# Attention and soft-mixture feed-forward on one core: the sums of the slots in three passes over high and low parts, in place of fp32

## What is computed

```python
x = layernorm(x + attention(x))            # x: 8 batches x 1024 tokens x 128
# feed-forward, per batch:
xn = rms_norm(x, gamma_x)                  # 1024 x 128
se = rms_norm(slot_embeds, gamma_slot)     # 512 slots x 128
logits = einsum('bsd,etd->bset', xn, se)   # 1024 tokens x 512 slots
dispatch = softmax(logits, axis=1)         # over the tokens
slots = einsum('bsd,bset->betd', xn, dispatch)
h = gelu(slots @ w1); processed = h @ w2   # 128 -> 512 -> 128
combine = softmax(logits, over the slots)
out = einsum('bnd,bsn->bsd', processed, combine)
x = layernorm(x + out)
```

## Time and profile before

| what | value |
|---|---|
| median of 3 runs | 1963.05 us (1960.64 to 1964.24) |
| the profiled execution's own time | 1951.72 us |
| its span | 1949.9 us |
| PE busy over the span | 1777.2 us (91%) |
| DVE busy | 1577.5 us (81%) |
| ACT busy | 1240.9 us (64%) |
| POOL busy | 1081.5 us (55%) |
| one steady feed-forward batch | 41.44 us |

### The profile page before, as it was taken

The page is one execution under the profiler, slowest core; times in us unless marked ns, Lnnn a source line. Parts: engine busy times, 40 slices in busy tenths (PEclk is TensorE's granted clock), DMA queues, the critical chain, the costliest instruction groups (busy, mean ns, idle before and its releaser), DMA issues. The chain is left out here.

```text
span 1949.9 us, 33601 instructions
## 1 busy us (share of the span) xinstructions
PE 1777.2 (91%) x10556; PEld 1527.5 (78%) x10556; DVE 1577.5 (81%) x2926; ACT 1240.9 (64%) x2450; POOL 1081.5 (55%) x661
## 2 busy tenths in 40 slices
PE   4899989998999899989998999899999949999997
PEld 4788877887788778867887888688888837878886
DVE  3879987997899778978997789788889856777674
ACT  2767766776777667756776677577767615445553
POOL 3556655664666556555665556566656433455543
PEclk7999999999999999999999999999999979999999
DMA  3322232223222322232223222322233120111100
GB/s 105 80 60 82 66 87 57 75 66 89 66 66 66 87 66 66 66 89 66 66 66 87 66 66 66 87 66 66 74 82 82 48 81 22 46 42 32 35 19 22
DMA packets 69767, 127.90 MB, mean 66 GB/s; under 512 B 15456, under 2 KB 42080, under 8 KB 69600
## 3 DMA queue, kind: packets, MB, share of 16 engines
q1 hardware_dynamic: 68416, 124.81, 23.5%
q10 hardware_dynamic: 1184, 1.05, 0.2%
HBM read 50.07 MB, written 8.65 MB: 30 GB/s over the span
## 5 line engine op out<-in xcount | busy, mean ns | idle before, releaser
L448 ACT ACTIVATE probs<-ps_slot,neg_max 128x640 f32<-128x640 f32 (+7 forms) x512 | 379.1, 742 | 172.7 <-DVE neg_max L533 165.2
L533 DVE CUSTOM_DVE_ANT_0 ps_slot<-ps_slot,causal 128x640 f32<-128x640 f32 (+7 forms) x512 | 385.5, 753 | 39.5 <-PE ps_slot L57 38.5
L681 PE MATMUL ps_turn<-ident,probs 128*128 128x128 f32 x2304 | 339.0, 278 | 54.6 <-DVE pt_high L564 34.7
L681 PEld LDWEIGHTS ps_turn<-ident,probs 128*128 128x128 f32 x2304 | 264.9, 142 | 95.3 <-DVE pt_high L564 37.9
L55 PE MATMUL ps_slot<-k,q 128*128 128x512 f32 (+3 forms) x768 | 284.1, 370 | 39.3 <-DVE rot_q L549 38.6
L412 POOL TENSOR_TENSOR q<-rot_q,q 128x1024 fp32r<-128x1024 f32 x64 | 154.0, 2406 | 269.9 <-ACT q L465 269.9
L56 PE MATMUL ps_slot<-k,q 128*128 128x512 f32 (+3 forms) x768 | 267.3, 348 | 0.0
L57 PE MATMUL ps_slot<-k,q 128*128 128x512 f32 (+3 forms) x768 | 267.0, 348 | 0.0
L412 POOL TENSOR_TENSOR k<-rot_k,k 128x1024 fp32r<-128x1024 f32 x64 | 153.0, 2390 | 112.0 <-ACT k L465 111.8
L556 DVE TENSOR_TENSOR rot_k<-rot_k,swapped_k 128x1024 f32<-128x1024 f32 x64 | 177.8, 2779 | 35.8 <-POOL swapped_k L404 35.8
L55 PEld LDWEIGHTS ps_slot<-k,q 128*128 128x128 f32 x768 | 145.9, 190 | 69.9 <-DVE rot_q L549 53.5
(11 more groups left out here) (165 smaller groups left out, 4551.8 us busy)
## 6 DMA issues: line engine op xcount, KB each, us to landing
swapped_k<-unrot_k SPq DMA_DIRECT2D x128, 256.0 KB, 3.6
swapped_q<-unrot_q SPq DMA_DIRECT2D x128, 256.0 KB, 3.7
inv_b<-inv_rows SPq DMA_DIRECT2D x64, 512.0 KB, 4.7
x_rows<-in_L_attn_x SPq DMA_DIRECT2D x8, 512.0 KB, 5.3
y_t<-y_sum SPq DMA_DIRECT2D x8, 512.0 KB, 3.4
y_in<-y_t SPq DMA_DIRECT2D x7, 512.0 KB, 3.7
x_row<-in_L_attn_x SPq DMA_DIRECT2D x7, 512.0 KB, 4.9
out<-out_row SPq DMA_DIRECT2D x7, 512.0 KB, 3.2
```

The source lines that it names most:

```text
L448: act.activation(probs_tile(t), score_tile(name, head, i), ACT.Exp, scale=-1.0, bias=neg_max[:, head.par, t:t + 1], accum_out=sums[:, head ...
L533: dve.tensor_tensor_reduce(tile, tile, causal[:, T - WIDTH[t]:T], -1.0, UNSEEN, ALU.add, ALU.min, neg_max[:, head.par, t:t + 1]).then_inc( ...
L681: last = pe.transpose(bank[:, at:at + P], probs_tile(t)[:, j * P:(j + 1) * P], ident[:, :])
```

## The change

`disp` becomes two parts of type fp32r, high and low, and `z_row` gets a copy in two such parts, `z_split` (`z_s`). ACT now empties all eight dispatch banks into the high part (`split_disp_hi`); DVE subtracts that high part from the same bank into the low part (`split_disp_lo`), and only then is the bank free for PE. ACT also makes the high part of the token rows (`split_z_hi`), POOL the low part (`split_z_lo`). `sum_slots` runs as `matmul_split`. The combine side, banks 8 to 15, stays as it was.

```diff
-        disp = s.sb("disp", [P, NT, N], F32)
+        disp = s.sb("disp", [P, 2, NT, N], F32R)
+        z_s = s.sb("z_split", [P, 2, NT, D], F32R)
...
+            def split_z_lo(b, par):
+                wait_apart(pool, z_hi, b + 1, ticks)
+                pool.tensor_tensor(z_s[:, 1, :, :], z_row[par][:, :, :], f32(z_s[:, 0, :, :]),
+                                   ALU.subtract).then_inc(z_lo, 1)
...
-                for i in range(8):
+                for i in range(4):
+                    norm_rows(b, i)
+                split_z_lo(b, par)
+                for i in range(4, 8):
                     norm_rows(b, i)
...
+            def split_disp_hi(b, bank_no):
+
+                act.wait_ge(turned, b * 16 + (bank_no + 2))
+                act.activation(disp_part(bank_no, 0), turn_src(bank_no), ACT.Copy).then_inc(turn_hi, 1)
...
-                copy_turn(b, 0)
-                copy_turn(b, 2)
+                split_disp_hi(b, 0)
+                split_disp_hi(b, 1)
+                split_z_hi(b, par, first)
+                split_disp_hi(b, 2)
                 exp(b, 2)
+                split_disp_hi(b, 3)
                 exp(b, 3)
-                copy_turn(b, 4)
-                copy_turn(b, 6)
+                split_disp_hi(b, 4)
+                split_disp_hi(b, 5)
+                split_disp_hi(b, 6)
+                split_disp_hi(b, 7)
...
+            def split_disp_lo(b, bank_no):
+                dve.wait_ge(turn_hi, b * 8 + (bank_no + 1))
+                dve.tensor_tensor(disp_part(bank_no, 1), turn_src(bank_no), f32(disp_part(bank_no, 0)),
+                                  ALU.subtract).then_inc(copied[bank_no % 2], 1)
...
-                    last = pe.matmul(ps_acc[:, 0, :], z_row[par][:, t, :], disp[:, t, :],
-                                     start=t == 0, stop=t == NT - 1, skip_group_check=True)
+                    last = matmul_split(pe, ps_acc[:, 0, :], z_s[:, 0, t, :], z_s[:, 1, t, :],
+                                        disp[:, 0, t, :], disp[:, 1, t, :], t == 0, t == NT - 1)
...
+                pe.wait_ge(z_lo, b + 1)
```

More of the change, by code:

```diff
@@ L850, in ffn_block @@
         slots_summed, proc_summed = s.sem("slots_summed"), s.sem("proc_summed")
+        turn_hi, z_hi, z_lo = s.sem("turn_hi1"), s.sem("z_hi"), s.sem("z_lo")
         out_summed = s.sem("out_summed")
@@ L897, in half_cols, with disp_part @@
             return slice(half * T // 2, (half + 1) * T // 2)
+        def disp_part(bank_no, part):
+            c, half = bank_no // 2, bank_no % 2
+            return disp[:, part, 4 * half:4 * half + 4, c * P:(c + 1) * P]
         def turn_dst(bank_no):
-            if bank_no < 8:
-                c, half = bank_no // 2, bank_no % 2
-                return disp[:, 4 * half:4 * half + 4, c * P:(c + 1) * P]
             t = bank_no - 8
@@ L1060, in copy_turn, with split_z_hi @@
                 act.activation(turn_dst(bank_no), turn_src(bank_no), ACT.Copy).then_inc(copied[0], 1)
+            def split_disp_hi(b, bank_no):
+                act.wait_ge(turned, b * 16 + (bank_no + 2))
+                act.activation(disp_part(bank_no, 0), turn_src(bank_no), ACT.Copy).then_inc(turn_hi, 1)
+            def split_z_hi(b, par, first):
+                if first:
+                    act.wait_ge(first_z, 2)
+                else:
+                    act.wait_ge(z_made, b)
+                act.activation(z_s[:, 0, :, :], z_row[par][:, :, :], ACT.Copy).then_inc(z_hi, 1)
             def split_zt(fill_count, fill):
@@ L1081, in _, with batch @@
                    .then_inc(first_hi, 1)
-            def batch(b, first, ahead):
+            def batch(b, par, first, ahead):
                 if not first:
@@ L1108, in batch @@
                     split_zt(count(b, F_ZT), F_ZT)
[L1110 to L1113, removed]
+            batch(0, 0, True, True)
+            with act.Fori(0, B // 2 - 1) as pair:
+                batch(pair * 2 + 1, 1, False, True)
+                batch(pair * 2 + 2, 0, False, True)
+            batch(B - 1, 1, False, False)
             copy_proc(B - 1)
@@ L1237, in batch @@
                 x1_rows(par, range(NT // 2, NT))
-                copy_turn(b, 1)
+                split_disp_lo(b, 0)
+                split_disp_lo(b, 1)
                 rowmax(b, 2)
-                copy_turn(b, 3)
+                split_disp_lo(b, 2)
+                split_disp_lo(b, 3)
                 invert(b, 2)
@@ L1243, in batch @@
                 invert(b, 3)
-                copy_turn(b, 5)
+                split_disp_lo(b, 4)
+                split_disp_lo(b, 5)
                 if not first:
@@ L1248, in batch @@
                     add1(count(b, F_TOKENS), F_TOKENS, b + 2)
-                copy_turn(b, 7)
+                split_disp_lo(b, 6)
+                split_disp_lo(b, 7)
                 rowmax(b, 4)
@@ L1344, in turn, with sum_slots @@
                     last.then_inc(turned, 1)
-            def sum_slots(par, tiles):
+            def sum_slots(tiles):
                 for t in tiles:
-                    last = pe.matmul(ps_acc[:, 0, :], z_row[par][:, t, :], disp[:, t, :],
-                                     start=t == 0, stop=t == NT - 1, skip_group_check=True)
+                    last = matmul_split(pe, ps_acc[:, 0, :], z_s[:, 0, t, :], z_s[:, 1, t, :],
+                                        disp[:, 0, t, :], disp[:, 1, t, :], t == 0, t == NT - 1)
                 return last
@@ L1427, in batch @@
                     pe.wait_ge(added2, b)
-                sum_slots(par, range(NT // 2))
+                pe.wait_ge(z_lo, b + 1)
+                sum_slots(range(NT // 2))
                 turn(b, 4)
@@ L1431, in batch @@
                 rows(6)
-                sum_slots(par, range(NT // 2, NT)).then_inc(slots_summed, 1)
+                sum_slots(range(NT // 2, NT)).then_inc(slots_summed, 1)
                 turn(b, 5)
```

## The result

The changed kernel takes 1968.95 us (median of 20 runs, 1962.04 to 1978.59), the kernel before, measured beside it, 1963.7 us (20 runs, 1957.77 to 1969.04). The ratio is 1.0033, with a 95% interval of 1.0019 to 1.0046: slower by a third of a per cent. The prediction was 1969.0. The difference of the two medians is 5.25 us, that of the two means 6.4.

What follows compares the result with a forecast made beforehand. PE bounds the kernel with DVE only 0.43 us behind; DVE's list becomes the bound. Six steady batches +5.8, batch 0 +0.6, batch 7 -0.4: 1963.05 + 6.0 = 1969.0 us, range 1960 to 1977, the forecast's own 1966 to 1972.

Steps and rivals of the forecast that it cites:

- PE's gain of 1.26 a batch: In two sum_slots calls a batch, twelve split matmuls take 2.80 us instead of 3.43 for four fp32 ones.
- PE can give no more than 0.43: From rows(4) to the last maximum, DVE waits for PE only 0.21 and 0.22 us, capping a batch's gain.
- A subtraction costs 0.60 on DVE, written 0.68: Each of eight subtractions replacing four DVE copies costs 0.60 us, like a copy; 2.4 us more a batch.
- The batch grows by 0.96: Steady batch: maximum of rows(4) 1.39 us late, less 0.43 of vanished waits for PE.
- The new wait of 1.2 us for bank 3, with all the rest queued behind: DVE waits 1.2 us before subtracting bank 3, which ACT empties only after the exponential of chunk 2.
- Batch 7 -0.4: Last batch, without add1 and first statistics: PE keeps its second call's gain less a small delay, -0.4 us.
- Batch 0 +0.6, since DVE has more room there: First batch, with neither add2 nor the second statistics, grows by only 0.6 us.
- The sum, 6.0: Whole kernel 6.0 us slower: +5.8 for six steady batches, +0.6 for batch 0, -0.4 for batch 7.
- About 3.4 us of DVE's waits ahead of 1703.54: DVE's idle time before the maximum of rows(4), said to exceed the 2.4 us of added subtractions.
- rival 2: Subtractions fall into DVE's waits ahead of rows(4)'s maximum; 1960 us, or 1963 if DVE is 0.43 late; chance 0.17.
- Where PE waits: PE's gain goes into waits: about 0.4 us before rows(5), 0.4 to 0.7 in turn(4), about 1 before the first hidden.
- Rival 1: PE stays the bound and its full 1.26 us a batch arrive, 1953.0 us in all; chance 0.07.

Runs made afterwards that it cites:

- three passes alone: Kernel before with only the slot sums as three passes, each multiplying high by high, no work added to other engines; 40.97 us a steady batch, ratio 0.998.
- Bank 3 early: Changed kernel with ACT's high part of bank 3 ahead of the exponential of chunk 2, that of the token rows behind it; 42.46 us a batch, ratio 1.0028.
- costs alone: Changed kernel with all its splitting work, but the slot sums in fp32 as before, over the high parts; 42.45 us a batch, ratio 1.0051.
- banks 9 and 11 on ACT: Kernel before with only the copies of combine banks 9 and 11 moved from DVE to ACT; 41.43 us a batch, ratio 1.0005.
- add2 first: Changed kernel with DVE's residual sum add2 moved ahead of the subtractions of banks 4 and 5; 42.03 us a batch, ratio 1.0032.
- rearranged lists: Changed kernel with bank 3's high part early, add2 ahead of banks 4 and 5, copies of banks 9 and 11 on ACT; 41.36 us a batch, ratio 1.0004.
- one pass: Kernel before with slot sums in one fp32r pass over high parts, banks 9 and 11 copied by ACT; 40.61 us a batch, ratio 0.9966.

## Why the prediction was right, step by step

- *PE's gain of 1.26 a batch*: the split matmuls do start 0.23 apart, 2.80 for twelve against 3.43. Right.
- *PE can give no more than 0.43*: 0.46 with three passes alone. Right.
- *A subtraction costs 0.60 on DVE, written 0.68*: 1703.30 to 1704.50 for two, written 0.68. Right. POOL's took 2.39 and was ready at 1714.5, ahead of the sums at 1716.54. It was never waited for.
- *The batch grows by 0.96*: 1.03. The two points it was built from are 1.54 (predicted 1.39) and 1.02 (0.96). The 0.15 between 1.39 and 1.54 is a term that the replay left out: it let PE reach `turn(2)` at its old time, and the subtraction of bank 1 holds PE in `turn(1)` for 0.15.
- *The new wait of 1.2 us for bank 3, with all the rest queued behind*: the wait is there, 1.16, but in batches 1 to 6 it is not what costs. That step was wrong in what it named, and right in its sum only because the replay already let DVE wait for bank 4. Bank 3 early changed nothing, and taking out two subtractions ahead of `turn(2)` gave 0.15. What costs is behind `turn(2)`, which PE reaches only 0.15 late: two subtractions more (1.10 when taken out) and the way over ACT to the first of them (0.2). The 1.0 us of added work said to vanish in waits is the work on banks 0 to 3.
- *Six steady batches +5.8*: +6.1 measured. *Batch 7 -0.4*: -0.7 (55.89 against 56.60 from its first maximum to the end).
- *Batch 0 +0.6, since DVE has more room there*: too small, as far as single traces can tell. Four traces reach `turn(0)` alike, 4.15 to 4.16 us behind the first maximum, and can be compared: before 40.14, three passes alone 39.15, costs alone 42.66, changed 41.69. That is +1.55, with the parts adding up (-0.99 and +2.52). The step that failed is that only DVE's room was looked at. PE waits for chunk 2 in this batch, and the late reciprocal goes straight into that wait (2.86 against 1.77); another 0.34 is waited in `turn(1)` for DVE, and the granted clock falls behind the long wait (last section).
- *The sum, 6.0*: the traces give 6.1 + 1.55 - 0.7 = 7.0, the medians 5.25, the means 6.4. That 1969.0 met the median of 1968.95 is luck to that digit: the kernel before measured 1963.7 beside the changed one, not 1963.05, and batch 0 was priced too low. The forecast for the profiled execution, 1957.7, missed by 9.4: it assumed an execution as far under the median as the one of the kernel before.
- *About 3.4 us of DVE's waits ahead of 1703.54* (rival 2): the written ones are 0.40, 0.68, 1.27 and 1.45, 3.8 in all. The 0.40 was left out; nothing else in the forecast uses this sum.
- *Where PE waits*: ahead of `rows(5)` 0.3, in `turn(4)` 0.3 and between its banks, ahead of `hidden` 0.7, as named, with less at the last than the 1 us given. A wait of 0.17 for DVE's bank at `turn(3)` and the 0.15 in `turn(1)` were not named.
- Rival 1 is out: with nothing added to the other engines, 0.46 of PE's 1.26 us arrived; with PE relieved by 5.0 and DVE by 1.2, 0.82. The Trainium skill (Perfetto Trace Analysis, Identifying the Most-Contended Engine) says to optimize the engine with the highest occupancy first. These traces bear it out only for the first 0.46 us.
- Rival 2 would need the subtractions to be hidden. Those ahead of `turn(2)` are, but for 0.15, and those behind are not, though by sum there was idle time enough ahead of 1703.54.

## What to carry to other kernels

Before work is taken off an engine that is busy all the time, look for how long the second engine's list waits for it in one round: that, not the work removed, is the most it can give. Count added work by where it stands: ahead of a wait for an engine that comes at a fixed time it is free as far as it does not hold up that engine itself (here 0.15 of 1.2 us came through), behind the wait it counts in full, and idle time elsewhere in the round does not help. A wait that shows in the trace is a cause only if the next wait does not take its place; moving it is a cheap test. Do the replay for the first and the last round too: the same wait cost nothing in six rounds and about 1 us in the first.

## What the hardware showed unexpectedly

Batch 0 varied more than a steady batch changed. The kernel before and the same with banks 9 and 11 on ACT have the same waits of PE there (2.80 us ahead of `turn(0)`, about 1.8 ahead of `turn(2)`), and took 40.14 and 42.66 us; the changed kernel and that with add2 first have the same code for it, and took 41.69 and 42.73. In the first pair all of the 2.5 us is lost by `turn(1)`, which starts 6.49 and 9.15 us behind the first maximum. The granted clock in the first us of batch 0 of the kernel before with banks 9 and 11 on ACT:

```profile
1608.00:1612.00 4.00, 3.87 (x11) 2.69 (x10) 2.05 (x5) 0.60 (x1) 0.00 (x0) 0.50 0.02 4
1612.00:1616.00 4.00, 2.26 (x6) 1.32 (x4) 2.76 (x5) 1.65 (x3) 0.20 (x1) 0.75 0.00 0
1616.00:1620.00 4.00, 2.94 (x12) 2.65 (x13) 3.74 (x9) 1.36 (x3) 2.21 (x2) 0.68 0.00 0
```

A granted clock of 0.50 is the level of 1.2 GHz. PE comes there from the start of the block, where it mostly waits for DMAs and DVE (13.5 and 8.9 us between 1574 and 1604 in the kernel before). The clock rose and then fell again for part of the time between 1616 and 1620, around PE's wait of 2.80. In the kernel before's own trace it was at 1.00 from 1605.56 on. So a trace's batch 0 tells of the clock in that execution as much as of the kernel, and the main comparison is that of batches 1 to 6, at 1.00 throughout.

Behind the longer wait that the change puts ahead of `turn(2)` the clock fell too. The changed kernel, around its wait of 2.86 up to 1625.47:

```profile
1624.00:1629.00 5.00, 3.53 (x19) 3.53 (x20) 2.95 (x7) 2.29 (x4) 3.26 (x3) 0.70 0.00 0
```

From `turn(2)` to the next batch's first maximum it took 29.22 us, against 28.38 in the kernel with bank 3 early, which waited 1.95 and was at 1.00 there. With the sums in fp32 it is 30.18 (costs alone, wait of 2.86, clock down to 0.71) against 29.34 (before, wait of 1.77, clock 1.00). The difference is 0.84 us in both pairs, and the instructions of PE are slower there (`turn(2)` written 1.47 and 1.43, against 1.10 and 1.09), so I put it down to the clock.

DVE's scaling of four `z_row` tiles takes 1.10 to 1.24 us while POOL is idle for most of it, and more while POOL scales two rows of 512 columns: 1.60 in the same batch of the kernel before (1719.19, POOL's scaling from 1718.84 for 1.37), 1.83 in the rearranged lists, 1.94 with one pass. The subtraction that reads PSUM was not slowed: of the pair at 1711.42 in the changed kernel the second ran beside POOL's subtraction of 2.39 us, and the pair took 1.29, as the others did (1.28). One such subtraction a batch is all that overlaps there.
